# A two-stage sequence kernel on one core: five of the 32 half-states of each batch scaled by ScalarE and summed by accumulating transfers

## What is computed

```python
def step(h, inp):
    d_t, B_t, C_t, u_t = inp
    dA = jnp.exp(d_t[:, :, None] * A[None])
    h = dA * h + (d_t * u_t)[:, :, None] * B_t[:, None, :]
    y = jnp.sum(h * C_t[:, None, :], axis=-1)
    return (h, y)
...
y = jnp.transpose(ys, (1, 0, 2)) + u * D_param
y = y * jax.nn.silu(z)
return y @ W_out
```

## Time and profile before

| what | before |
|---|---|
| median of 3 runs | 4104.61 us |
| profiled execution | 4102.7 us |
| its span | 4100.8 us |
| VectorE busy | 2738.9 us (67%) |
| TensorE busy | 3529.0 us (86%) |
| ScalarE busy | 2036.7 us (50%) |
| GpSimd busy | 1899.9 us (46%) |
| mean granted TensorE clock | 0.907 |

### The profile page before, as it was taken

The page is one execution under the profiler, slowest core; times in us unless marked ns, Lnnn a source line. Parts: engine busy times, 40 slices in busy tenths (PEclk is TensorE's granted clock), DMA queues, the critical chain, the costliest instruction groups (busy, mean ns, idle before and its releaser), DMA issues.

```text
span 4100.8 us, 36398 instructions
## 1 busy us (share of the span) xinstructions
PE 3529.0 (86%) x12362; PEld 1915.2 (47%) x12362; DVE 2738.9 (67%) x3491; ACT 2036.7 (50%) x3486; POOL 1899.9 (46%) x1142
## 2 busy tenths in 40 slices
PE   5799999999999999767888888888888888888858
PEld 1445455454545454344454454444444544444543
DVE  1343434343434343279899799899898897997992
ACT  1233333333333333474676667656655755766542
POOL 1021212121221212195676677667667756767760
PEclk8899999999999999867889889898899898898859
DMA  5001010101010101111213222222222132121111
GB/s 197 34 1 44 1 44 0 44 1 44 1 44 1 44 11 62 38 42 61 73 63 98 67 73 82 73 84 80 65 90 80 63 113 70 62 96 59 42 59 41
DMA packets 100937, 230.04 MB, mean 56 GB/s; under 512 B 10305, under 2 KB 10417, under 8 KB 97682
## 3 DMA queue, kind: packets, MB, share of 16 engines
q1 hardware_dynamic: 97186, 220.50, 16.1%
q10 hardware_dynamic: 3568, 7.21, 0.5%
HBM read 193.85 MB, written 33.83 MB: 56 GB/s over the span
## 4 chain that ended last, share of the span: by engine, by line
PE 18%; POOL 14%; DVE 12%; issue 12%; ACT 3%; DMA 0%; POOLq 0%; SPq 0%; DVEq 0%; ACTq 0%
POOL HS L1181 10%; PE bank L1542 10%; DVE HS L1420 6%; DVE acc L1425 5%; PE bank L1618 3%; PE bank L1559 3%; PE bank L1616 1%; POOL delta L1196 1%; POOL ZS L1187 1%; DVE U L1457 1%; POOL DU L1199 1%; ACT bank L1258 1%; POOL comb L1212 1%; PE bank L1568 0%; POOL comb L1215 0%
## 5 line engine op out<-in xcount | busy, mean ns | idle before, releaser
L1181 POOL TENSOR_TENSOR HS<-DU,brep 128x1024 f32<-128x1024 f32 x512 | 1197.5, 2357 | 635.8 <-PE bank L1559 635.8
L1420 DVE TENSOR_TENSOR_SCAN HS<-bank,HS 128x1024 f32<-128x1024 f32 x512 | 1167.8, 2281 | 71.2 <-ACT bank L1258 58.5
L1559 PE MATMUL bank<-ident,HS 128*128 128x128 f32 x4096 | 686.9, 319 | 342.0 <-DVE acc L1425 307.0
L1258 ACT ACTIVATE bank<-delta,aneg 128x511 f32<-128x511 f32 x1024 | 662.1, 680 | 501.6 <-DVE HS L1420 499.5
L1559 PEld LDWEIGHTS bank<-ident,HS 128*128 128x128 f32 x4096 | 559.0, 164 | 617.7 <-DVE HS L1420 401.4
L447 POOL TENSOR_TENSOR PR<-PR,rrec 128x512 f32<-128x512 f32 x256 | 260.4, 1041 | 1264.5 <-DVE rrec L713 1264.5
L1425 DVE SCALAR_TENSOR_TENSOR acc<-bank,C,acc 128x512 f32<-128x512 f32 x960 | 667.1, 737 | 135.4 <-PE bank L1559 133.9
L1542 PE MATMUL bank<-XM,w_l 128*128 128x512 f32 x1024 | 498.9, 635 | 43.1 <-DVE U L1457 19.1
L1542 PE MATMUL bank<-w_l,G 128*128 128x512 f32 x1024 | 476.6, 611 | 7.3 <-ACT delta L1268 3.9
L530 ACT ACTIVATE PR<-bank,nsmax 128x512 f32<-128x512 f32 x256 | 174.7, 685 | 425.1 <-DVE nsmax L709 419.8
L780 PE MATMUL bank<-w_l,NT 128*128 128x512 f32 x768 | 355.0, 607 | 5.6 <-ACT NT L478 5.5
(11 more groups left out here) (171 smaller groups left out, 4007.5 us busy)
## 6 DMA issues: line engine op xcount, KB each, us to landing
brep<-b_d SPq DMA_DIRECT2D x256, 256.0 KB, 3.2
w_l<-in_L_cond_W_in SPq DMA_DIRECT2D x14, 2048.0 KB, 9.7
w_l<-in_L_cond_W_full SPq DMA_DIRECT2D x8, 2048.0 KB, 8.6
w_l<-in_L_cond_W_out SPq DMA_DIRECT2D x7, 2048.0 KB, 9.7
X<-in_x SPq DMA_DIRECT2D x8, 1024.0 KB, 5.2
x_d<-X SPq DMA_DIRECT2D x8, 1024.0 KB, 4.8
xm_d<-XM SPq DMA_DIRECT2D x8, 1024.0 KB, 4.3
ot_d<-OT SPq DMA_DIRECT2D x8, 1024.0 KB, 3.8
```

The lines of the kernel that those rows point to most:

```text
L1181: nc.gpsimd.tensor_tensor(HS[:, u % DEEP], DU[:, chunks(j, s), :], brep[:, m % 3, :].unsqueeze(1).to_broadcast([P, UC, T]), ALU.mult).then ...
L1258: last = nc.scalar.activation(dA[:, s, i, 1:T], delta[:, c, 1:T], ACT.Exp, scale=aneg[:, c, n:n + 1])
L1420: nc.vector.tensor_tensor_scan(h, dA[:, u % 2].rearrange("p i t -> p (i t)"), h, 0.0, ALU.mult, ALU.add).then_inc(scanned, 1)
L1559: last = nc.tensor.transpose(y_bank[t % 2][:, i * P:(i + 1) * P], h, ident[:])
```

## The change

Five of the 32 half-states of each batch are taken from VectorE: n = 2, 11 and 13 in half 0, n = 6 and 8 in half 1. For these, ScalarE multiplies the turned bank by the column of C into a scratch place (`scale_spared`, one slot after the turn, right behind that slot's decay), in half 0 in XM, in half 1 in the right half of comb. GpSimd then issues a transfer from the scratch to acc that adds (`sum_spared`, two slots after the turn, ahead of that slot's product), one for two blocks, 128 partitions x 1024 elements. A bank is free when ScalarE has scaled it. VectorE's sum of the next state waits for the transfer of its pair of blocks. Because XM is now scratch during half 0, the load of the next batch's XM moves from SyncE's slot 1 to slot 28 of half 0, behind a wait for these transfers.

```diff
-        TURNED, ADDED = (N + 1) * TT, (N - 1) * TT
+        TURNED = (N + 1) * TT
+        SPARED = ((2, 11, 13), (6, 8))
...
-        SP_B, SP_OUT, SP_OT, SP_GATE, SP_XM, SP_PROJ, SP_FULL = 16, 13, 14, 10, 1, 27, 1
+        SP_B, SP_OUT, SP_OT, SP_GATE, SP_XM, SP_PROJ, SP_FULL = 16, 13, 14, 10, 28, 27, 1
...
+        def spared(j, n):
+            return j // 2 * sum(map(len, SPARED)) + j % 2 * len(SPARED[0]) + sum(m < n for m in SPARED[j % 2])
+
+        def added(j, n):
+            return (j * (N - 1) + max(n - 1, 0) - spared(j, n)) * TT
+
+        def emptied(j, n, t):
+            if n == 0:
+                return sum_begun, j * TT + t + 1
+            if n in SPARED[j % 2]:
+                return scaled, spared(j, n) * TT + t + 1
+            return acc_done, added(j, n) + t + 1
+
+        def scratch(j, t):
+            return XM[:, t:t + 1, :] if j % 2 == 0 else comb[:, t:t + 1, D:2 * D]
+
+        def scratch_pair(j, k):
+            return XM[:, 2 * k:2 * k + 2, :] if j % 2 == 0 else comb[:, 2 * k:2 * k + 2, D:2 * D]
...
                 def load_xm(n):
+                    if n:
+                        for k in range(2):
+                            sp.wait_ge(summed[k], spared(2 * n - 1, 0) * 16)
                     sp.dma_start(XM[:], xm_d[n]).then_inc(xm_in, 16)
...
+                def sum_spared(j, s):
+                    n, k = s // 2, s % 2
+                    if s < 0 or n not in SPARED[j % 2]:
+                        return
+                    pool.wait_ge(scaled, spared(j, n) * TT + 2 * k + 2)
+                    pool.wait_ge(*emptied(j, n - 1, 2 * k + 1))
+                    nc.gpsimd.dma_start(acc[:, 2 * k:2 * k + 2, :], scratch_pair(j, k), accum_op=ALU.add).then_inc(summed[k], 16)
...
                     for s in range(SLOTS):
+                        sum_spared(b * 2, s - 2)
                         dbu(b * 2 * UNITS + s + 4)
...
+                        sum_spared(b * 2 + 1, s - 2)
                         dbu((b * 2 + 1) * UNITS + s + 4)
...
+                def scale_spared(j, s):
+                    b, n, k = j // 2, s // 2, s % 2
+                    if s < 0 or n not in SPARED[j % 2]:
+                        return
+                    if j % 2 == 0:
+                        act.wait_ge(ring.full, ring.at(b, "z7"))
+                    else:
+                        after(act, out_ready, b * TT)
+                    after(act, summed[k], spared(j, n) * 16)
+                    for t in (2 * k, 2 * k + 1):
+                        act.wait_ge(yt_full, j * TURNED + n * TT + t + 1)
+                        nc.scalar.activation(scratch(j, t), y_bank[t % 2].unsqueeze(1), ACT.Identity, scale=C[:, b % 2, t, n:n + 1]).then_inc(scaled, 1)
...
                     act.wait_ge(ring.full, ring.at(b, f"p{t}"))
+                    act.wait_ge(summed[t // 2], spared(2 * b + 2, 0) * 16)
...
+                        scale_spared(b * 2, s - 1)
                         if p is not None:
                             tail(p, s)
...
+                        scale_spared(b * 2 + 1, s - 1)
                         if p is not None:
                             tail(p, s + SLOTS)
...
                 def add(j, n, pair):
+                    if n in SPARED[j % 2]:
+                        return
+                    if n - 1 in SPARED[j % 2]:
+                        dve.wait_ge(summed[pair[0] // 2], spared(j, n) * 16)
...
-                    elif k < TT + 2:
-                        pe.wait_ge(sum_begun, j * TT + k - 1)
                     else:
-                        pe.wait_ge(acc_done, j * ADDED + k - TT - 1)
+                        pe.wait_ge(*emptied(j, (k - 2) // TT, (k - 2) % TT))
```

More of the change, by code:

```diff
@@ L976, in mix @@
         dA_done, scanned, dbu_done = sem("dA_done"), sem("scanned"), sem("dbu_done")
+        scaled, summed = sem("scaled"), [sem(f"summed{k}") for k in range(2)]
         yt_full, sum_begun, acc_done, tot_done, g_done = sem("yt_full"), sem("sum_begun"), sem("acc_done"), sem("tot_done"), sem("g_done")
@@ L1562, in total @@
                 def total(j):
-                    pe.wait_ge(acc_done, (j + 1) * ADDED)
+                    pe.wait_ge(acc_done, added(j, N))
                     for i in range(HC):
```

## The result

| what | before | after |
|---|---|---|
| median | 4105.05 us (5 runs, 4102.66 to 4108.52) | 4145.29 us (5 runs, 4132.55 to 4150.58) |
| ratio after/before | | 1.0095, 95% interval 1.0076 to 1.0113 |
| profiled execution | 4102.7 us | 4148.59 us |
| its span | 4100.8 us | 4146.8 us |
| VectorE busy | 2738.9 us | 2639.0 us |

What follows compares the result with a forecast made beforehand. VectorE is busiest in the scan stage, but ScalarE and TensorE set the pace in several spared slots. Profiled 4102.7 + 4.7 (turns) + 5.6 (transfers) = 4113.0 us, 4115 on the median; 8-in-10 range 4070 to 4165.

Steps and rivals of the forecast that it cites:

- ScalarE's and TensorE's turns: Scan stage: VectorE's 104 us saving goes to these engines' turns, not the end; sum before transfers +4.7 us.
- signs of being wrong: Half 1 not longer, sums waiting over 1 us each for DMA, or TensorE's clock falling where full (2.6 us per product).
- n=13: Half 0, slots 26 and 27: ScalarE has room; slot 30's scan 2.8 us earlier, 0.9 from n=11 included; landings cost 0.6.
- Transfers: Ten accumulating 512 KB transfers per batch: landing waits of 0.6 at n=13 and 0.2 at n=6, 5.6 us in all.
- L: Time from a GpSimd transfer's issue to its landing, taken as 5.2 us.
- Rival B: Slow landings of 7.5 us, if descriptors wait for a running scan: 4164 us in all; chance 0.20.
- Half 1, n=6 and n=8: Scalings delay ScalarE's decay, then the relu TensorE waits for: n=6 loses 0.9 us, half 1 ends 3.65 us later.
- Half 0, n=2: Slots 4 and 5: scalings delay softplus(4)'s relu by 2.2 us, so slot 6's sums come later: +0.45 us.
- The ends: Half 0 of batch 0 changes by 0; half 1 of batch 7, without front, gains 4.4 us.
- The counts: VectorE's sums 800, ScalarE's scalings 160, GpSimd transfers 80.
- GpSimd's issue: Issuing each accumulating transfer takes 1.1 us of GpSimd's time, hidden because it is ahead by two products.
- The moved load: XM's load in slot 28 lands at 17.7 us, TensorE wants it at 17.6: cost 0, no cover left.

Runs made afterwards that it cites:

- e7: The changed kernel with its accumulating transfers not issued, waits for them replaced by waits for the scalings: 4093.79 us, ratio 0.9971 to the kernel before.
- e3: The changed kernel with only n=11 of half 0 spared: 4126.78 us, ratio 1.0059 to the kernel before.
- e8: The changed kernel with only n=11 spared and the next batch's W_in load moved from SyncE's slot 24 to 27: 4107.77 us, ratio 1.0008 to before.
- e9: The changed kernel with only n=13 of half 0 spared, run once more in five rounds: 4081.16 us, ratio 0.9942 to the kernel before.
- e2: The changed kernel with only n=13 of half 0 spared, first time: 4083.92 us, ratio 0.9954 to the kernel before.
- e1: The changed kernel with no state spared, leaving the late load of XM and the moved code: 4103.9 us, ratio 0.9998 to the kernel before.
- e5: The changed kernel with only n=6 of half 1 spared: 4110.07 us, ratio 1.0013 to the kernel before.
- e10: The changed kernel with n=13 spared in all halves 0, plus n=8, 10 and 12 in the last half: 4083.71 us, ratio 0.9944 to the kernel before.
- e6: The changed kernel with only n=8 of half 1 spared: 4123.33 us, ratio 1.0044 to the kernel before.

## Why the prediction was right, and where its sum was wrong

The sign and the likeliest case were right, and 4145 lies in the range, but the sum said +10 and it is +40. In part the sign was luck. The forecast laid the loss on ScalarE's and TensorE's turns, +4.7, and with the scalings alone (e7) the kernel is 10.5 us faster than before: what makes the change a loss is the term that the forecast put at 5.6. Two of the prediction's own signs of being wrong came true as well, sums that wait over 1 us for a DMA, and a product that runs at the low clock where it ran at full. The five states measured alone give -20.1 (n=13), +22.7 (n=11), +6.8 (n=2), +5.7 (n=6) and +19.0 (n=8), each median less its own before: +34 together, so they are nearly additive and one can judge them one at a time.

- **Transfers: the step that failed.** "At n=11 and 8 nothing below 6.5. So 0.8 x 7 = 5.6 us." The step took one L for all places. L as such was well placed: 5.8 in the median for 5.2 forecast, 4.5 to 5.1 in most batches at n=13. But at n=11 it is 10.4 to 12.3 in the six batches that load W_in in the same slot. The term was 5.6 and measured 51 (full change less e7): 28.9 in halves 0, shown by e3 against e8 to be mostly this collision, 6.0 in halves 1, and 14 at the two ends, where the sum had nothing for transfers. "Nothing below 6.5" at n=11 fails besides: in batch 0 a landing of 6.7 us (5.9 in e3) was waited for by 5.2 us (4.9). The issue of W_in at slot 24 stands in SyncE's list of slots; I went through that queue for the load that was moved and not for what else would be on the wires. The trace before had the price too, in the x1 block that took 8.8 us beside W_in for 3.5 elsewhere; the earlier trace rows show medians, which hide it.
- **Rival B** came near with its 4164, 19 above, but by another mechanism. It asked for slow landings everywhere, from descriptors that wait for a scan. Landings of 4.5 to 5.1 us at n=13 start beside scans too, so no such conflict is seen. (The 2357 ns that the prediction gives for 512 products stand for 484 in the earlier trace rows; the page of all 512 has the same mean.) GpSimd's product went from 2357 ns to 2408 on average, 51 x 485 = 25 us in the scan stage, or 0.32 us for each of its 78 issues; a product that begins right behind an issue takes 2.65 us for 2.36, so the issues would explain this too.
- **Half 1, n=6 and n=8.** Right in mechanism and nearly in size: 3.1 us per half for 3.65 and 0.2. n=6 lost what it saved in slot 13, to the table load's queue (3.9 us of waiting for ScalarE there), and slots 12 to 15 add 1.1 us for 0.85 forecast (the wait stands in slot 13, from scan to scan, where I had written 14). At n=8 the forecast put all four scalings on the path; slots 16 to 21 add 2.2 for 2.8. Without transfers (e7) the half is only 2.3 us longer, so the ScalarE part was forecast 1.4 us too large per half, 10 us in seven. With the transfers come 0.9 per half; more than half of it lies in slots 1, 2 and 30, far from the spared states, and is not explained.
- **Half 0, n=2.** The forecast said +0.45; it is +0.4 in halves at full clock. The 2.6 us for a slow product that the prediction named as what would make it wrong did happen, in two of the seven halves: 5.97 us for 3.70.
- **n=13.** Predicted -1.9 and +0.6 for landings; slots 26 to 28 give -2.1 in the full change and -2.4 in e9, since its transfers land in 4.5 to 5.2 us in most batches. With batch 0 that is 18.5 us; the medians say 20 (e2) and 26 (e9). What is above 18.5 lies at the ends of the halves, where TensorE's clock shifts, and isn't taken apart.
- **The ends.** The last half was forecast 4.4 us shorter and is 1.0 longer. In e7 it is 5.5 shorter, so the landings took 6.5. Most of that is one more collision: n=6's transfers, issued around the 1 MB load of the attention output, took 8.3 and 9.7 us and that load 9.2 for its 6.5, and slot 14 is 5.3 us longer, with 5.23 us of waiting for the landing. No run moved that load, so this one is argued from the trace and from e3 and e8. Half 0 of batch 0 was forecast at 0; it is +1.7 in the full change and -5.5 in e7, by the landings of n=11 and n=13 in quiet slots. The first scan also starts 2.8 us later in the profiled run after. It is 1.6 to 4.1 us later in e1 to e5, e9 and e10, 0.5 in e7, and 2.7 and 3.0 earlier in e6 and e8, so this moves from run to run, and no step of the sum reaches there.
- **The counts** came as forecast: 800 sums by VectorE, 48 + 32 transfers, 160 scalings.
- **GpSimd's issue.** Forecast 1.1 us, hidden. Measured 0.87 and 1.20 in the median, with 1.7 us at most, and hidden: its idle time fell from 630 to 540 us. **The moved load**: forecast 0, measured 0 (e1).

Summed, ScalarE's side came out 15 us better than its +4.7 (e7 is 10.5 below before) and the transfers 45 worse. The two errors hid part of each other, and the median of 4145 alone wouldn't have told that.

## What to carry to other kernels

When an engine is relieved by a transfer, price the transfer at the place it is issued, with the list of every other transfer in flight there: the same 512 KB took 4.5 us in one slot and 12 in another. Look for a small transfer that is already slow at that place; a median over all of its kind hides it. Take moved work apart by site and time each site alone before all are switched on; here one of five sites paid 20 us and the others took it away more than twice over. And a queue in program order hands a new instruction's delay to all behind it: at n=6 the 2.6 us saved on VectorE bought 3.85 us of waiting for the decay that stood behind the scaling.

## What the runs showed of the hardware

- An accumulating transfer of 512 KB within the on-chip memory takes 4.5 us at least and 5.8 in the median of the full change's 80 from its issue by GpSimd to landing. The Trainium skill's rule for a GpSimd-issued transfer ("DMA: Bandwidth & Descriptors", section "Anatomy of one DMA", 2.0 us and the bytes at 436 GB/s) would give 3.2, as an estimate. No transfer here was as fast.
- Beside a 2 MB load it takes 10.4 to 12.3 us in the full change, the load goes from 9.6 to 10.0 us to 15.0 to 15.4, and a 256 KB block issued right behind goes from 7.9 to 9.0 us to 11.3 to 12.0 (3.5 in the median of all such blocks). Beside a 1 MB load it took 8.3 and 9.7 us (the last half of the full change) and 10.5 and 9.9 (e10).
- GpSimd spends 0.87 us in the median (0.83 to 1.20) on issuing one whose source rows are contiguous (XM) and 1.20 us (1.17 to 1.68) where each partition's source is two pieces of 2 KB (comb). The two kinds also stand at different places of the schedule, and no run separates this.
- The phase of TensorE's granted clock moves with small shifts of the work. A product of eight 128x512 matmuls takes 3.6 to 3.7 us at full clock and 5.3 to 6.8 us where the granted clock over the product itself is 0.54 to 0.69 (kernels before and after). So a gain or loss of 2 to 4 us in one half is not to be put down to an edit before the clock of the stretch is read.
